# Reordering the first chunk of a three-pass f32 projection phase: keys by contraction tile, x on the sync queue, rows normalised earlier, identity products ahead

## The reference

```python
x = x + tanh(g_xattn) * attention(layernorm(x), ctx, ctx, adj, mask, Wq, bq, Wk, bk, Wv, bv, Wo, bo)
x = x + tanh(g_ffn) * coupled_ffn(layernorm(x), cn_w1..4, gc_w1..3, adaptive_range)

def attention(query, key, value, ...):          # 16 heads of 32
    Q = heads(query, Wq, bq); K = heads(key, Wk, bk); V = heads(value, Wv, bv)
    scores = Q @ K.T / sqrt(32) + adj
    scores = where(mask == 0, -inf, scores)
    return softmax(scores) @ V @ Wo.T + bo
```

## Time and profile before

| | us |
|---|---|
| median of 3 runs | 1820.77 |
| lowest and highest run | 1819.86, 1821.71 |
| the profiled execution | 1819.01 |
| its span | 1817.2 |
| PE busy in the span | 1761.7 (97%) |

### The profile page before, as it was taken

How to read it: one execution, slowest core, us unless ns; L and a number is a source line. 1 busy time by engine, 2 the same in 40 slices (tenths; PEclk the granted TensorE clock), 3 DMA queues, 4 the chain that set the end, 5 groups by cost and what they waited for, 6 DMA issues and landing times. The chain is left out here.

```text
span 1817.2 us, 33693 instructions
## 1 busy us (share of the span) xinstructions
PE 1761.7 (97%) x12280; PEld 1274.7 (70%) x12280; DVE 1458.7 (80%) x2527; ACT 1220.3 (67%) x2121; POOL 653.2 (36%) x591
## 2 busy tenths in 40 slices
PE   7999999999999999999999999999999899899896
PEld 6888886777777777777777777777764664755752
DVE  5545555999999999999999999999658847847848
ACT  3222225999999999999999999999454344443542
POOL 3432423332387442586324864633242110110100
PEclk9999999999999999999999999999999999999998
DMA  8777666745478653667753777526315330330101
GB/s 263 264 252 281 249 231 171 169 144 129 130 186 180 135 138 94 181 172 134 164 120 100 206 164 151 116 73 174 104 47 174 107 93 1 107 93 0 61 1 46
DMA packets 152212, 254.60 MB, mean 140 GB/s; under 512 B 17024, under 2 KB 69504, under 8 KB 152064
## 3 DMA queue, kind: packets, MB, share of 16 engines
q1 hardware_dynamic: 101408, 157.73, 27.0%
q0 software_dynamic: 50080, 93.87, 23.4%
q10 hardware_dynamic: 576, 1.05, 0.2%
HBM read 168.44 MB, written 84.15 MB: 139 GB/s over the span
## 5 line engine op out<-in xcount | busy, mean ns | idle before, releaser
L967 DVE CUSTOM_DVE_ANT_0 a_neg<-a_sc_ps,am 128x1024 f32<-128x1024 f32 x512 | 621.1, 1213 | 1.3 <-PE a_sc_ps L820 1.3
L916 ACT ACTIVATE a_prob<-a_neg,a_row_min 128x1024 f32<-128x1024 f32 x512 | 586.6, 1146 | 7.7 <-DVE a_row_min L967 4.6
L832 PEld LDWEIGHTS a_tr_ps<-ident,a_prob 128*128 128x128 f32 x4096 | 460.4, 140 | 136.1 <-issue 100.3
L832 PE MATMUL a_tr_ps<-ident,a_prob 128*128 128x128 f32 x4096 | 545.8, 276 | 1.4 <-ACT a_probT L896 1.4
L942 DVE COPY a_probT<-a_tr_ps 128x512 f32<-128x512 f32 x512 | 353.8, 691 | 49.0 <-PE a_tr_ps L832 36.5
L896 ACT ACTIVATE a_probT<-a_tr_ps 128x512 f32<-128x512 f32 x512 | 305.6, 597 | 74.2 <-PE a_tr_ps L832 49.1
L1293 PE MATMUL f_acc<-f_u,f_w 128*128 128x512 f32 x384 | 173.5, 596 | 0.0
L716 POOL DMA_DIRECT2D a_q_st<-q_parts x144 | 79.4, 557 | 210.1 <-PE a_sc_ps L820 174.3
L853 PE MATMUL a_o_ps<-a_probT,v_first 128*32 128x256 f32 x2048 | 137.0, 385 | 0.0
L853 PE MATMUL a_o_ps<-a_probT,a_v 128*32 128x256 f32 x2048 | 136.4, 385 | 0.2 <-ACT a_probT L896 0.2
L1293 PEld LDWEIGHTS f_acc<-f_u,f_w 128*128 128x128 f32 x384 | 71.4, 190 | 90.7 <-issue 75.8
(11 more groups left out here) (202 smaller groups left out, 2964.0 us busy)
## 6 DMA issues: line engine op xcount, KB each, us to landing
a_q_st<-q_parts POOLq DMA_DIRECT2D x144, 128.0 KB, 2.9
k_first<-k_parts POOLq DMA_DIRECT2D x24, 512.0 KB, 7.8
a_k_st<-k_parts POOLq DMA_DIRECT2D x24, 512.0 KB, 7.5
a_m_raw<-mask SPq DMA_DIRECT2D x24, 512.0 KB, 5.2
a_adj_raw<-adj SPq DMA_DIRECT2D x24, 512.0 KB, 6.6
p_x_raw<-x POOLq DMA_DIRECT2D x8, 1024.0 KB, 7.4
k_parts<-p_out_hi SPq DMA_DIRECT2D x32, 256.0 KB, 3.2
k_parts<-p_out_lo SPq DMA_DIRECT2D x32, 256.0 KB, 5.6
```

Of the source, the lines that this page charges most:

```text
L832: last = pe.transpose(tr_ps[:, half, j * P:(j + 1) * P], prob[:, r % NPROB, t * P:(t + 1) * P], ident[:])
L916: act.activation(prob[:, r % NPROB, :], neg[:, r % 2, :], ACT.Exp, scale=-1.0, bias=row_min[:, r % 2:r % 2 + 1], accum_out=row_sum[:, r // ...
L967: dve.tensor_tensor_reduce(out=neg[:, r % 2, :], in0=sc_ps[:, r % 2, :], in1=am[:, 2 * qb + qt, :], scale=-1.0, scalar=3.4e38, op0=ALU.add ...
```

## The change

Only chunk 0 changes, in six places:

1. x's first load moves from POOL's queue to SP's, behind the two bias loads and ahead of the load of `bv_rows` and the gates. It waits for the third context tile as it did on POOL, and has a semaphore of its own.
2. PE makes 10 products of the identity with itself into `x_t` before anything else, as soon as the identity is there.
3. The keys of chunk 0 go by contraction tile: for each of the 4 tiles, all four banks (12 matmuls) before the next tile's data is waited for.
4. On DVE `norm_stats(0)` and `norm_apply(0)` come straight after the tile splits, ahead of the scaling of `bias_q` and of weight 1's split.
5. On ACT and DVE weight 2's split comes after the key banks are read.
6. DVE waits for its own last weight split before it writes `v_out`.

```diff
@@ gpsimd
             pool.wait_ge(c_tile_loaded[ET - 2], 16)
-            pool.dma_start(x_raw[:], x[0:CH].rearrange("(t p) e -> p t e", p=P)).then_inc(x_loaded, 16)
             for n, array in ((1, WvT), (2, WqT)):
@@ sync
                 sp.dma_start(bias_k[:], bk.rearrange("(t p) -> p t", p=P)).then_inc(b_loaded, 16)
+                sp.wait_ge(c_tile_loaded[ET - 2], 16)
+                sp.dma_start(x_raw[:], x[0:CH].rearrange("(t p) e -> p t e", p=P)).then_inc(first_x_loaded, 16)
                 sp.dma_start(bv_rows[:], bv.partition_broadcast(P)).then_inc(b_loaded, 16)
@@ tensor
+            def first_keys():
+                pe.wait_ge(acc_read, 4)
+                for t in range(ET):
+                    pe.wait_ge(c_lo_ready, t + 1)
+                    pe.wait_ge(w_lo_ready, t + 1)
+                    for m in range(4):
+                        ms = slice(m * P, (m + 1) * P)
+                        last = three_pass(pe, acc[:, m, :], w_hi[:, 0, t, ms], w_lo[:, 0, t, ms], c_hi[:, t, :], c_lo[:, t, :], t == 0, t == ET - 1)
+                        if t == ET - 1:
+                            last.then_inc(acc_ready, 1)
...
+            pe.wait_ge(id_ready, 1)
+            for n in range(10):
+                pe.matmul(x_t[:, 0, 0:P], ident[:], ident[:], start=True, stop=True)
             chunk(0, True)
@@ scalar
             split_weight(1)
-            split_weight(2)
...
                 high_parts(c, 0, bias_k)
+                if isinstance(c, int) and c == 0:
+                    split_weight(2)
@@ vector
+            norm_stats(0)
+            norm_apply(0)
             dve.wait_ge(b_loaded, 48)
             dve.tensor_scalar(bias_q[:], bias_q[:], INV_SQRT_D, None, ALU.mult).then_inc(bq_scaled, 1)
             dve.wait_ge(bq_scaled, 1)
-            norm_stats(0)
             split_weight(1)
-            norm_apply(0)
-            split_weight(2)
...
                 low_parts(c, 0, 0, bias_k)
+                if isinstance(c, int) and c == 0:
+                    split_weight(2)
...
+                if isinstance(c, int) and c == 0:
+                    dve.wait_ge(w_lo_ready, 3 * ET)
```

More of the change, by code:

```diff
@@ L208, in project_phase @@
         x_loaded = sem("p_x_loaded")
+        first_x_loaded = sem("p_first_x_loaded")
         c_loaded = sem("p_c_loaded")
@@ L339, in chunk @@
                 xs = (xT_hi, xT_lo)
-                for m in range(4):
-                    w = lambda part, t: (w_hi, w_lo)[part][:, 0, t, m * P:(m + 1) * P]
-                    product(c, m, w, lambda part, t: cs[part][:, t, :]).then_inc(acc_ready, 1)
                 if first:
-                    pe.wait_ge(id_ready, 1)
+                    first_keys()
+                else:
+                    for m in range(4):
+                        w = lambda part, t: (w_hi, w_lo)[part][:, 0, t, m * P:(m + 1) * P]
+                        product(c, m, w, lambda part, t: cs[part][:, t, :]).then_inc(acc_ready, 1)
                 pe.wait_ge(xn_ready, c + 1)
@@ L419, in norm_stats @@
             def norm_stats(c):
-                dve.wait_ge(x_loaded, 16 * (c + 1))
+                if isinstance(c, int) and c == 0:
+                    dve.wait_ge(first_x_loaded, 16)
+                else:
+                    dve.wait_ge(x_loaded, 16 * c)
                 for s in range(TT):
```

## The result

The changed kernel takes 1824.62 us (median of 15 runs, 1820.25 to 1828.15), the kernel before 1820.57 (15 runs, 1817.38 to 1822.82): a ratio of 1.0024, interval 1.0016 to 1.0032. That is 4.05 us more, just past the 0.2% (3.6 us) that the prediction set as its bound, and the interval reaches from 2.9 to 5.8 us. In the profiled executions the span went from 1817.2 us to 1822.6, 5.4 more. Later medians are each set beside the kernel before as it ran in the same comparison: 1820.79 us for experiments 1, 3, 6 and 7, 1819.77 for 2, 4, 5 and 8. The ratio given with each is made from runs lying side by side, and differs a little from the quotient of the two medians.

What follows compares the result with a forecast made beforehand. PE, busy 1761.7 of 1817.2 us, bounds the kernel, so chunk 1's key start decides. That start +1.1 and the slow clock +1.8 make +2.9: 1820.77 + 2.9 = 1823.7 us, range 1819.8 to 1827.0.

Steps and rivals of the forecast that it cites:

- the case beyond it: Slower outcome, over +3.6 us: x landing late, or full store-load collisions and a longer slow clock; chance 0.37.
- Identity products, keys by tile: PE in chunk 0: clock rises before the keys, which end at about 17.6 instead of 19.8; worth nothing by itself.
- x on SP's queue: Program start: x's first load, issued on SP at about 7.1, lands at 12.4 instead of 14.83.
- x lands late: Rival: x lands after 13.1, delaying chunk 1 undiminished; at 14.2, 1825.5; 0.37 shared with full collisions and longer slow clock.
- Rows ahead of the split: DVE in chunk 0: normalised rows ready at 18.7 instead of 23.7, weight 1's low part only 0.65 us earlier.
- T: Moment weight 1's low part is done on DVE: x's landing plus 8.8, forecast 21.2 instead of 21.85.
- The mask: First mask tile's load, now beside eight key stores: delayed 0 to 1.2 us, 0.3 taken.
- v_all in the load's way: Chunk 0's values store, at 34.2, meets chunk 1's context load: 0 to 2.7 us later, 2.4 taken.
- The bank's release: DVE frees the query bank for chunk 1's keys 6.75 us after the context lands, at 50.15.
- The clock behind the wait: PE runs slow after its 6.1 us wait ahead of chunk 1's keys: 1.8 us lost, 0.8 to 2.6 allowed.
- The cover of 0.9 us: In the kernel before, the context-to-bank chain at chunk 1 is only 0.9 us earlier than PE's own.
- the full gain: Rival: chunk 1 starts at 44.0 against 49.05, 1815.7; needs the context by 37.3; chance of any faster result 0.05.

Runs made afterwards that it cites:

- experiment 1: Changed kernel with POOL's loads of chunk 1's context and x issued early, ahead of the first mask tile; 1815.14 us against 1820.79, ratio 0.9973.
- experiment 3: Changed kernel without the ten identity products; 1823.92 us against 1820.79, ratio 1.0016.
- experiment 6: Changed kernel with chunk 0's key stores held until the mask landed and v_all's until chunk 1's context landed; 1822.08 us against 1820.79, ratio 1.0009.
- experiment 7: Changed kernel with 26 more identity products between chunk 0 and chunk 1, to fill PE's wait; 1823.17 us against 1820.79, ratio 1.0012.
- experiment 2: Kernel before the change, with chunk 1's context and x loads issued early as in experiment 1; 1820.93 us against 1819.77, ratio 1.0001.
- experiment 4: Kernel of experiment 1 without the ten identity products; 1814.43 us against 1819.77 (6 runs), ratio 0.9968.
- experiment 5: Kernel of experiment 1 with x's first load back on POOL's queue, ahead of WvT; 1816.96 us against 1819.77, ratio 0.9986.
- experiment 8: Changed kernel with 34 identity products in PE's wait ahead of chunk 1; 1822.54 us against 1819.77, ratio 1.0015.

## Why the prediction came out as it did

Forecast 1823.7 (+2.9), measured 1824.62 (+4.05), with the range 1819.8 to 1827.0. The mechanism on record is the one that ran: TensorE gains at the start and gives it back waiting for chunk 1's context. Two of its terms were too small, the mask's and, a little, the clock's. The size lies between the forecast case (+1.3 to +3.6) and the case beyond it (0.37), just inside the second. By its own steps:

- **Identity products, keys by tile: right.** Keys fast from the second on, ended at 17.7 (17.6 said); worth nothing, in the changed kernel and in the faster one (experiments 3 and 4). That they may fail to raise the clock, and that it costs nothing, came true too (experiment 6's profile).
- **x on SP's queue: right in kind, 0.7 us short.** 12.4 said, 13.12 measured. SP issued it at 7.45 instead of 7.1, since the context tile that it waits for landed later, and it took 5.7 us instead of 5.3. That is on the very edge of the rival "x lands late" (from 13.1), but not its mechanism: experiment 5 shows that the queue gained 1.8 to 2.0 us, and not the 0.6 which that rival's far end took, and WvT, expected beside x from 10 us on, moved nothing between 8.5 and 12.5.
- **Rows ahead of the split: right.** T = x + 8.8 held (13.12 + 8.82 = 21.94). As x was 0.7 late, T did not gain at all, and xn was ready at 17.56 + 1.92 = 19.5 instead of 18.7.
- **The mask: the step that failed.** 0 to 1.2 us were allowed for the key stores and 0.3 taken; it was 2.0, above the upper end. Its ground isn't borne out either: experiment 6 had no stores and was 1.3 us late too, and what makes the mask late stays open. The bounds were drawn around one cause, and the spread of the transfer itself was never asked for.
- **v_all in the load's way: right in size, wrong in order.** 2.4 said and 2.1 measured, and experiment 6 takes them away. But the prediction took from the earlier trace rows that POOL's queue wins where both are full, and here the opposite happened: the store ran first and alone. That the size came out all the same is partly luck. The range of 0 to 2.7 hid the mistake, and experiments 3, 7 and 8 show about the same cost with the load ahead.
- **The bank's release: right.** From context to bank 6.75 said, 51.61 + 0.68 - 45.57 = 6.72 measured.
- **The clock behind the wait: right in kind, 0.4 us short.** 1.8 said (0.8 to 2.6 allowed), 5.66 - 3.44 = 2.2 measured: the nine products make 1.8, and the first interval nearly 0.4. By the same marks it was 1.7 in experiment 7, 2.5 in experiment 3 and 2.9 in experiment 6, so the upper bound was too low as well.
- **The cover of 0.9 us: right.** Experiment 2, the early loads without the change, found nothing.

The misses of chunk 1's start add up: 0.7 for T, 1.7 for the mask, -0.3 for v_all, and 0.2 between the bank's release and TensorE's start, 2.3 together; 52.49 - 50.15 = 2.34. With them and the clock's 2.2 the sum would have been +5.6, as chunk 2's 5.66 in the profiled execution, but over the medians' 4.05. The forecast of +2.9 is 1.2 us from the medians' difference and 2.8 from this execution's, and that it is so near the former is in part luck: the steps that can be read missed by more. Part of the difference may be the mask: experiments 3 and 8 landed it in 4.5 us, so its 2.0 us need not be in every run. But experiment 3 shows that an early mask alone gives nothing back where the adj tile and the normalisation are late instead. What was not predicted is the spread between executions of a load that nobody else disturbs. The median fell into the case of late x, or full collisions and a longer slow clock. Of these x and the clock came true by a little (0.7 and 0.4 us), v_all's collision did not exceed the forecast, and the largest miss was the mask's 1.7.

One rival was never a contender: the full gain. It needed the context by 37.3, and no row allowed that in this order of POOL's work. Experiment 1 made just that true, with 5 us gained in place of 4 lost.

## What to carry to other kernels

Where two chains end within a microsecond of each other, a gain on one is worth that microsecond and no more; find out what the second one waits for and start that first, here a load that sat behind a tile of mask work that it does not need. Moving work earlier also moves its stores, so ask which load they will now meet. And bound a transfer's time by how it varies between rows of the same transfer, not only by the one neighbour that might disturb it.

## What the runs showed of the hardware

- A pause as short as 2.88 us, right behind 6 us of identity products, was followed by 3.4 us at half clock, which fell only after TensorE was back at work. Those of 3.47, 3.71 and 4.04 us (experiments 5 and 2, the kernel before) came with 3.4 us too, that of 4.92 us (experiment 6) with 6.8 and those of 7.6 and 7.7 us with 10.2, a part of it inside the pause. What it cost did not grow with the pause: 1.7 us behind 2.88, 2.9 behind 4.92, 2.2 behind 7.70. Behind pauses of up to 1.87 us it did not fall.
- Ten products of two passes each, on an identity, between 1.5 and 6 us gave fast keys in five of six profiles (0.23 us a product against 0.43 without), and in the sixth nine slow keys as without them; 34 of them held the granted clock at 1.00 through a wait.
- The same 1 MB of x at the program's start landed 5.1 to 5.7 us after its issue on SP's queue (seven profiles) and 7.1 to 7.6 on POOL's (three), and the difference went through to the total (1814.43 and 1815.14 against 1816.96).
- Of a 1 MB store on SP's queue and a 1 MB load on POOL's, issued within 0.1 us, the store, issued first, took all 16 engines (100.9% of 36 to 39 us); where the load was issued 0.9 us ahead (experiment 3), it had 84.1% of the same stretch and the store nothing. Neither queue always goes first.
- The same 512 KB load took between 4.5 and 6.55 us in six profiles, once with its last packets trickling at 6% of the engines and nothing else under way on SP's queue. Its cause is open.
- VectorE's normalisation of 512 rows took 2.63 to 2.73 us in the three profiles in which GpSimd's mask instruction ran beside it, and 1.91 in the seven in which it didn't (chunk 1's rows in each).
